# Row maxima handed over once a sequence instead of once a half, in a macaron block's attention

## The reference

```
x = x + 0.5 * ffn(layernorm(x))     # ternary weights, 1024 hidden units, silu(up) * gate
x = x + attn(layernorm(x))          # 16 heads of 16, 4 key/value groups, causal softmax
x = x + 0.5 * ffn(layernorm(x))
```

## Time and profile before

| | us |
|---|---|
| median of 3 runs | 615.65 |
| the runs | 616.25, 613.38, 615.65 |
| profiled execution, its own time | 613.52 |
| its span, first to last instruction | 611.8 |
| outputs of group 0 begin | 222.8 |
| outputs of chunk 6's first group begin | 397.8 |
| the attention's last output copy ends | about 441 |

### The profile page before, as it was taken

One profiled execution on the slowest core, in us unless ns is written; L12 is line 12 of the kernel. 1 busy time (PEld: TensorE's weight loads), 2 busy tenths in 40 slices (PEclk: granted clock), 3 DMA queues, 4 the chain that ended last, 5 costly groups with the idle time before them and its releaser, 6 DMA issues.

```text
span 611.8 us, 12440 instructions
## 1 busy us (share of the span) xinstructions
PE 566.2 (93%) x4276; PEld 344.7 (56%) x4276; DVE 484.4 (79%) x1850; ACT 413.2 (68%) x780; POOL 185.3 (30%) x231
## 2 busy tenths in 40 slices
PE   2879999999989889999899989998899999999998
PEld 2335566655656755666565656554445556666666
DVE  6797988889976789888988887888298687856654
ACT  4746656765645268898889888887866656665741
POOL 3022301101420234555555454557741011101100
DMA  9601101100203250514141414230111211212112
GB/s 313 211 19 34 19 18 35 35 19 18 36 0 96 46 143 6 140 36 108 54 91 56 90 56 90 81 65 5 36 35 34 53 53 36 66 49 59 35 35 70
DMA packets 69503, 37.90 MB, mean 62 GB/s; under 512 B 33856, under 2 KB 66880, under 8 KB 69440
## 3 DMA queue, kind: packets, MB, share of 16 engines
q1 hardware_dynamic: 69440, 37.11, 23.8%
HBM read 18.22 MB, written 10.49 MB: 47 GB/s over the span
## 4 chain that ended last, share of the span: by engine, by line
PE 76%; DVE 11%; ACT 8%; issue 2%; DMA 2%; SPq 1%; DVEq 0%; ACTq 0%
PE bank L1076 31%; PE bank L1088 16%; PE bank L1175 7%; PE bank L1239 6%; PE bank L1230 5%; PE bank L1202 5%; PE bank L1253 2%; PE bank L1244 2%; ACT shared L568 2%; DVE sm_out L938 2%; DVE hl L821 2%; DVE hid L806 2%; DVE stats L692 1%; PE bank L1213 1%; PE bank L1067 1%
## 5 line engine op out<-in xcount | busy, mean ns | idle before, releaser
L938 DVE CUSTOM_DVE_ANT_0 sm_out<-bank,mask 128x256 f16<-128x256 f32 (+1 forms) x512 | 153.0, 351 | 29.4 <-PE bank L1202 27.5
L464 ACT ACTIVATE silu<-bank,w_scale 128x512 f32<-128x512 f32 x128 | 87.4, 683 | 114.7 <-PE bank L1076 114.7
L806 DVE SCALAR_TENSOR_TENSOR hid<-silu,h_unit,bank 128x512 f32<-128x512 f32 x128 | 95.0, 742 | 64.5 <-ACT silu L464 64.1
L568 ACT ACTIVATE shared<-bank,qk_scale 128x512 f32<-128x512 f32 x192 | 121.3, 675 | 22.6 <-PE bank L1230 22.0
L1088 PE MATMUL bank<-wT_down,hh 128*128 128x256 f16 x512 | 118.3, 273 | 7.4 <-DVE hl L821 6.0
L1088 PE MATMUL bank<-wT_down,hl 128*128 128x256 f16 x512 | 118.2, 273 | 0.0
L821 DVE TENSOR_TENSOR hl<-hid,hh 128x512 f16<-128x512 f32 x128 | 103.2, 806 | 0.0
L1076 PE MATMUL bank<-xh,wT_up 128*128 128x512 f16 x256 | 98.0, 383 | 4.9 <-issue 2.5
L396 POOL TENSOR_TENSOR xnl<-xn,xnh 128x1024 f16<-128x1024 f32 x14 | 30.1, 2152 | 236.0 <-ACT xn L495 223.5
L1076 PE MATMUL bank<-xl,wT_up 128*128 128x512 f16 x256 | 98.0, 383 | 0.0
L1076 PE MATMUL bank<-xh,wT_gate 128*128 128x512 f16 x256 | 97.3, 380 | 0.8 <-DVE hid L806 0.7
(11 more groups left out here) (111 smaller groups left out, 751.5 us busy)
## 6 DMA issues: line engine op xcount, KB each, us to landing
q_st<-q_scratch SPq DMA_DIRECT2D x32, 256.0 KB
q_scratch<-q_hl SPq DMA_DIRECT2D x8, 512.0 KB, 3.1
out_dram<-x SPq DMA_DIRECT2D x7, 512.0 KB, 2.9
x<-in_x_dram SPq DMA_DIRECT2D x1, 3072.0 KB, 15.5
k_scratch<-k_hl SPq DMA_DIRECT2D x16, 128.0 KB, 2.4
k_st<-k_scratch SPq DMA_DIRECT2D x16, 128.0 KB
x<-in_x_dram SPq DMA_DIRECT2D x2, 512.0 KB, 4.3
shared<-in_w_up_t_dram SPq DMA_DIRECT2D x2, 512.0 KB, 6.6
```

The costliest lines, as they stand in the source:

```text
L464: act.activation(silu[:, e % 2, :], U[e % 2][:, :], ACT.Silu, scale=w_scale[:, 0:1]).then_inc(silu_ready, 1)
L568: act.activation(prob[:, place % 2, i, :], ST[(3 * place + i) % 2][:, :], ACT.Exp, scale=qk_scale[:, 4:5]).then_inc(exp_done, 1)
L806: dve.scalar_tensor_tensor(out=hid[:, e % 4, :], in0=silu[:, e % 2, :], scalar=h_unit[:, 0:1], in1=GT[e % 2][:, :], op0=ALU.mult, op1=ALU. ...
L938: ins = dve.tensor_tensor_reduce(sm_out[:, i, cols], SM[i][:, cols], mask[:, S - size:S], 1.0, MASKED, ALU.add, ALU.max, rowmax[:, seq_par ...
```

## The change

Everything that was done for 8 heads at g = 0 and g = 2 is done for 16 heads at g = 1. `HH` goes; `mx_hl` becomes [16, 2, 256], `mx_32` [16, 256], `mx_loaded` one semaphore. The transposes stand inside the group, after its `max_scores` and ahead of its third `scores`; ScalarE's copies stand between the second and the third exp; `outputs` now also waits for those copies; GpSimd's subtraction stands ahead of the selects. `max_scores` runs seven groups ahead. The projection pieces end one group earlier. Keys and the two query halves are written by separate steps, each as soon as it is ready, and the rows are cleared by the first of the four reads. The first maxima are turned over after the first feed-forward.

```diff
@@ SP @@
+            def write_queries(c, par, m):
+                sp.wait_ge(qkv_lo, 3 * c + m + 2)
+                sp.dma_start(q_scr[par, :, :, :, m]..., q_hl[:, :, m, :]).then_inc(scr_written, 16)
...
             def read_scratch(c, par, seq):
                 sp.wait_ge(scr_written, 16 * N_SCR * (c + 1))
+                sp.dma_start(q_st[64:66, par, :, cols], q_st[66:68, par, :, cols]).then_inc(loaded, 16)
                 for n in range(2):
...
-                sp.dma_start(q_st[64:66, par, :, cols], q_st[66:68, par, :, cols]).then_inc(loaded, 16)
...
-                        if g in (0, 2) and not (last and k == 3):
-                            load_max(b + 1, k + 1, g // 2)
+                        if odd and g == 0 and not last:
+                            write_queries(c + 2, par, 0)
+                        if g == 1 and not (last and k == 3):
+                            load_max(b + 1, k + 1)
+                        if not odd and g == 3 and not last:
+                            write_keys(c + 2, par)
                         if odd and g == 1 and not last:
-                            write_scratch(c + 2, par)
-                        if odd and g == 2 and not last:
+                            write_queries(c + 2, par, 1)
                             sp.wait_ge(st_ready, 3 * G * b)
                             read_scratch(c + 2, par, 0)
+                        if odd and g == 2 and not last:
                             sp.wait_ge(st_ready, 3 * G * (b + 1))
                             read_scratch(c + 2, par, 1)
@@ POOL, attention_pair @@
+                        if g == 1 and not end:
+                            max_rest(b + 1)
                         if not (end and g == 3):
                             causal(4 * b + g + 1, (g + 1) % 2)
-                        if g in (0, 2) and not end:
-                            max_rest(b + 1, g // 2)
@@ ACT, attention_pair @@
-                            if odd and g == 1:
+                            if odd and g == 0:
                                 query_high(c + 2, 1)
                         if not (end and g == 3):
-                            exps(*ahead, range(1, 3))
+                            exps(*ahead, range(1, 2))
+                        if g == 1 and not end:
+                            max_copy(b + 1)
+                        if not (end and g == 3):
+                            exps(*ahead, range(2, 3))
...
                         act.wait_ge(pv_ready, n + 1)
-                        if g in (0, 2) and not end:
-                            max_copy(b + 1, g // 2)
                         act.activation(oT[:, odd, g, :], PV[:, 0:S], ACT.Copy).then_inc(oT_ready, 1)
@@ ACT, attention @@
                 query_high(1, 0)
-                max_copy(0, 0)
+                max_copy(0)
                 query_high(1, 1)
-                max_copy(0, 1)
@@ DVE @@
-                            if odd and g == 1 and i == 2 and not last:
+                            if odd and g == 0 and i == 2 and not last:
                                 query_low(c + 2, 1)
...
-                for n in (4, 5):
+                for n in (4, 5, 6):
                     first_row_max(n)
-                row_max(6, 1, 2, 0)
+                row_max(7, 1, 3, 0)
@@ PE @@
-            def max_transposes(b, k, half):
-                pe.wait_ge(sm_done, 3 * (G * b + 2 * half + 2))
...
+            def max_transposes(b, k):
+                pe.wait_ge(sm_done, 3 * G * (b + 1))
...
-            PLACES = [..., (2, 0), (2, 1), (2, 2), (3, 0), (3, 1), (3, 2), (4, 0), (4, 2), (5, 0)]
+            PLACES = [..., (2, 0), (2, 1), (2, 2), (2, 3), (3, 0), (3, 1), (3, 2), (3, 3), (4, 0)]
...
-                            if g == 2:
+                            if g == 1:
                                 pe.wait_ge(st_loaded[1 - par][odd], 16 * N_ST * (pair + par + 1))
...
                             max_scores(*lead, range(2, 3))
+                        if g == 1 and not end:
+                            pe.wait_ge(oT_ready, n + 1)
+                            max_transposes(b + 1, k + 1)
                         projection(2)
...
                         pe.wait_ge(oT_ready, n + 1)
-                        if g in (0, 2) and not end:
-                            max_transposes(b + 1, k + 1, g // 2)
+                        if g == 1 and not end:
+                            pe.wait_ge(mx_ready, b + 2)
                         outputs(n, k, g)
...
             def attention():
                 pe.wait_ge(st_loaded[0][1], 16 * N_ST)
+                max_transposes(0, 0)
                 max_scores(4, 1, 0)
-                pe.wait_ge(res_done, NT + 2)
-                max_transposes(0, 0, 1)
                 val_transposes(1, (qkv_lo, 5))
+                max_scores(5, 1, 1)
+                max_scores(6, 1, 2)
                 scores(0, 0, 0, 0)
-                max_scores(5, 1, 1)
-                max_scores(6, 1, 2, range(0, 1))
+                max_scores(7, 1, 3, range(0, 1))
+                pe.wait_ge(res_done, NT + 2)
```

More of the change, by code:

```diff
@@ L46, in macaron_block @@
     NT = NC * TT
-    HH = H // 2
     VW = 32
@@ L334, in causal, with max_rest @@
                                    pattern=[[0, HPG], [1, P]], channel_multiplier=-1).then_inc(prob_ready, 1)
[L336 to L342 removed]
+            def max_rest(b):
+                pool.wait_ge(mx_ready, b + 1)
+                if b:
+                    pool.wait_ge(mx_loaded, 32 * b)
+                pool.tensor_tensor(mx_hl[:, 1, :], mx_32[:, :], mx_hl[:, 0, :], ALU.subtract).then_inc(mxlo_ready, 1)
             def attention_pair(pair, last):
@@ L552, in val_copy, with max_copy @@
                                ACT.Copy).then_inc(val_ready, 1)
-            def max_copy(b, half):
-                act.wait_ge(mxT_ready, 2 * b + half + 1)
-                if not (isinstance(b, int) and b == 0):
-                    act.wait_ge(mx_loaded[half], 32 * b)
-                maxima = FIRST_MT if isinstance(b, int) and b + half == 0 else MT
-                act.activation(mx_hl[:, half, 0, :], maxima[0:HH, :], ACT.Copy, scale=-1.0 / MAX_UNIT)
-                act.activation(mx_32[:, half, :], maxima[0:HH, :], ACT.Copy,
-                               scale=-1.0 / MAX_UNIT).then_inc(mx_ready, 1)
+            def max_copy(b):
+                act.wait_ge(mxT_ready, b + 1)
+                if b:
+                    act.wait_ge(mx_loaded, 32 * b)
+                maxima = MT if b else FIRST_MT
+                act.activation(mx_hl[:, 0, :], maxima[0:H, :], ACT.Copy, scale=-1.0 / MAX_UNIT)
+                act.activation(mx_32[:, :], maxima[0:H, :], ACT.Copy, scale=-1.0 / MAX_UNIT).then_inc(mx_ready, 1)
             def exps(n, place, parts):
@@ L974, in attention_pair @@
                     for g in range(G):
-                        lead = (4 * b + g + 6, (k + (g + 6) // 4) % 2, (g + 2) % 4)
-                        ahead = not (last and (k == 3 or (k == 2 and g >= 2)))
+                        lead = (4 * b + g + 7, (k + (g + 7) // 4) % 2, (g + 3) % 4)
+                        ahead = not (last and (k == 3 or (k == 2 and g >= 1)))
                         steps = {(0, 3): range(0, 4), (1, 0): range(4, 8),
@@ L1206, in max_scores @@
                     ins.then_inc(sm_ready, 1)
-            def max_transposes(b, k, half):
-                pe.wait_ge(sm_done, 3 * (G * b + 2 * half + 2))
-                if not (isinstance(b, int) and b == 0 and half == 0):
-                    pe.wait_ge(mx_ready, 2 * b + half)
+            def max_transposes(b, k):
+                pe.wait_ge(sm_done, 3 * G * (b + 1))
+                if b:
+                    pe.wait_ge(mx_ready, b)
                 for qt in range(QT):
-                    ins = pe.transpose((FIRST_MT if isinstance(b, int) and b + half == 0 else MT)[0:HH, qt * P:(qt + 1) * P], rowmax[:, k % 2, qt, half * HH:(half + 1) * HH],
+                    ins = pe.transpose((MT if b else FIRST_MT)[0:H, qt * P:(qt + 1) * P], rowmax[:, k % 2, qt, :],
                                        ident32[:, :])
@@ L1219, in scores @@
                 par, seq = k // 2 % 2, k % 2
-                if g % 2 == 0 and 0 in parts:
-                    pe.wait_ge(mx_loaded[g // 2], 32 * (b + 1))
+                if g == 0 and 0 in parts:
+                    pe.wait_ge(mx_loaded, 32 * (b + 1))
                 at, heads = seq * S, slice(HPG * g, HPG * (g + 1))
@@ L1265, in attention_pair @@
                         n, end = 4 * b + g, last and k == 3
-                        lead = (n + 6, k + (g + 6) // 4, (g + 2) % 4)
-                        ahead = not (end or (last and k == 2 and g >= 2))
+                        lead = (n + 7, k + (g + 7) // 4, (g + 3) % 4)
+                        ahead = not (end or (last and k == 2 and g >= 1))
                         def projection(place):
```

52 lines of the change are left out of this document (25 added, 27 removed).

## The result

| | before | after |
|---|---|---|
| median of 4 runs | 615.51 | 622.12 |
| the runs | 613.38 to 616.25 | 619.61 to 625.37 |
| profiled execution, its own time | 613.52 | 619.61 |
| its span | 611.8 | 617.9 |
| outputs of group 0 begin | 222.8 | 226.5 |

After / before is 1.0122 with a 95% interval of 1.0094 to 1.0149: slower by 1.2%. The forecast was 614.5, in a range of 609.5 to 618.7, so it was wrong in sign and in size.

What follows compares the result with a forecast made beforehand. TensorE (93% busy) was taken as the bound, with ScalarE the chain in odd g = 1 and g = 3. +3.7 - 2.9 - 0.5 - 1.4 = -1.1 us, profile 612.4, median 614.5; range 609.5 to 618.7.

Steps and rivals of the forecast that it cites:

- start: Ahead of the pairs: maxima copies delay query_high(1, 1), VectorE does one more group before the first pair; sum +3.7 us.
- chunks 0 to 5: Plain chunk saves 0.19, chunks 0, 2, 4 save 0.78 with the earlier last queries; together -2.9 us.
- chunk 6: Last pair: g = 1 costs +0.47 twice, the six other groups lose 1.41 in all; net -0.5 us.
- chunk 7: Last chunk: g = 1 gets +0.23, g = 2 loses 0.72 and 0.38, g = 3 loses 0.49; -1.4 us.
- Spare falls from 2.1 to 0.1. I take 0.: Strip reads wanted by TensorE at even g = 1: cost taken as 0, bounds 0 and 2.0 a chunk.
- the first rival: Strips arrive late: TensorE waits at even g = 1, chunks 1 to 6; 0.9 a chunk costs 5.4, giving 619.9; chance 0.18.
- The 0.59 goes ... I take the whole.: Chunks 0, 2, 4: query_low at odd g = 0 removes VectorE's 0.59 lateness; bounds 0 and 0.59.
- Odd g = 1, 3.49.: Outputs to outputs in odd g = 1, waiting for copies behind the second exp: 3.49 us, +0.23 against 3.26.
- The wait for the copies: At g = 1 outputs wait for ScalarE's maxima copies behind the second exp; odd +0.23, even 0.2 after TensorE's 3.48.
- The rival "does not bite": ScalarE far enough ahead at g = 1 that outputs needn't wait for the copies: 8.0 more saved, 606.5; chance 0.14.
- The landing of the maxima's load, 0.7 spare.: Odd sequence: load lands about 3.1 us after the copies, needed at g = 3 after 3.8, so 0.7 spare.
- The rival of a cheaper start: TensorE ends the feed-forward earlier or VectorE's extra group hides: half of 3.7 goes, 612.6; chance 0.13.

Runs made afterwards that it cites:

- k5: Changed kernel with 14 spare matmuls on TensorE ahead of the pairs, where it waits for row maxima; 618.74 us, ratio 1.0075 to the kernel before.
- k10: Changed kernel with SP writing the second query half at odd g = 0, ahead of its wait for the maxima; 618.27 us, ratio 1.0060.
- k11: Changed kernel with the maxima's copies in their old place, ahead of the PV copy, so outputs need not wait for them; 626.51 us, ratio 1.0195.
- k2: Changed kernel with SP issuing a chunk's second strip read only once the first strip has landed; 622.86 us, ratio 1.0134.
- k7: Changed kernel with the edits of k4, k1, k5 and k6 together; 610.22 us, ratio 0.9935 to the kernel before.
- k3: Changed kernel with the last four layernorm steps of chunks 0, 2, 4 moved from odd g = 1 to odd g = 2; 622.31 us, ratio 1.0134.
- k6: Changed kernel with the layernorm steps moved from the odd sequence of chunks 0, 2, 4 to the even sequence of chunks 1, 3, 5; 619.04 us, ratio 1.0096.
- k4: Changed kernel with the maxima copied ahead of the second exp instead of behind it; 615.61 us, ratio 1.0018 to the kernel before.
- k1: Changed kernel with ScalarE's query_high(1, 1) ahead of max_copy(0) before the pairs; 620.82 us, ratio 1.0085 to the kernel before.
- k12: Kernel before with only the new projection-piece places and the last queries' two parts at odd g = 0; 617.98 us, ratio 1.0055.
- k8: Kernel before with only the layernorm steps moved to the even sequence of chunks 1, 3, 5; 612.79 us, ratio 0.9972.

## Why the prediction was wrong, step by step

The miss is 7.2 in the profiled span (6.1 measured, -1.1 forecast) and 7.6 in the medians. By stretch:

| term | forecast | measured | miss |
|---|---|---|---|
| start | +3.7 | +3.8 | 0.1 |
| chunks 0 to 5 | -2.9 | +2.0 | 4.9 |
| chunk 6 | -0.5 | +1.0 | 1.5 |
| chunk 7 | -1.4 | -0.7 | 0.7 |

By cause, in the same profile: late strips 2.8; ScalarE's path to the outputs of g = 1, 2.0; VectorE 1.4; the maxima's load 0.5. The rest, 0.5, is small differences. Without the late strips the change would still have been slower in the profile, by 3.3, so the strips are the largest term and not the whole cause.

- **"Spare falls from 2.1 to 0.1. I take 0."** This is the step that failed in kind, and it was the first rival. For chunks 1 to 5 the spare was sized about rightly, and with 0.1 of it the first longer write made a strip late by 1.43 (chunk 5). For chunk 6 it was sized wrongly: the 10.7 us until TensorE wants the strip holds an even g = 0 of 4.49, put in for all six chunks, and chunk 6's takes 3.77. That makes its strip late by itself (0.63 in k5, where write and issue took their usual time), and 1.35 with the long issue. The two are 2.8 in all, and 2.8 is what k10 took away. It is less than the rival's 0.9 a chunk, since only two of seven strips were late. In the experiments that keep after's order of writes chunk 6 is always late, by 0.6 to 1.6; with it are late, k11 aside, none to three of the others, not the same ones from kernel to kernel. The rival's reason (strips in competition) was wrong: k2. Chunk 0 of k7 apart, what makes the others late is a write, a read or an issue that takes longer than usual, and each of these has a 16 KB instruction packet beside it (below).
- **"The 0.59 goes ... I take the whole."** VectorE was called just level with 3.4 us of work in 3.6. It was not: odd g = 2 is 3.13 where the steps run and 2.65 where not, 0.48 three times, 1.4. k3 moved it and gained nothing, k6 took it away and gained 1.4 in its intervals. Of the bounds 0 and 0.59, the right end was 0.11.
- **Odd g = 1, 3.49.** It took 3.70. From the PV copy on the sum holds (2.64 forecast, 334.05 - 331.43 = 2.62 measured). The miss is ahead of it: the PV copy was put right behind the outputs, 0.85 after their start, and came at 1.08, because ScalarE was still in the third exp of the group before. ScalarE had no slack from the start of that group, so each piece on it counted. Together with even g = 1 (3.77, 3.68 forecast) that is 6 x (0.21 + 0.09) = 1.8, and 0.2 more in the last pair (3.31 for 3.24 twice, 3.09 for 3.00).
- **The wait for the copies.** It was forecast to bite, and does. Its full price was not worked out against the obvious other order. k4 says it: 6.4 us by the ratios for one exp ahead of the copies; of the 6.0 in the profile 4.3 came directly and the rest through the maxima's load and the strips, for which the copies are the first link. The rival "does not bite" forecast 8.0 for no wait at all.
- **The landing of the maxima's load, 0.7 spare.** It was late twice, 0.5 in all: in odd g = 3 of chunk 5 (2.92), behind the issue of 1.5, after which it landed 2.7 and not 1.8 to 1.9 from that issue; and 0.28 in chunk 7, where GpSimd's subtraction took 1.17 and not 0.67, and the load is wanted 3.4 after the copies and not 3.8. The 2.0 us that the prediction draws from the Trainium skill (DMA: Bandwidth & Descriptors, Anatomy of one DMA) is given there for DMAs issued from GpSimd; these are issued from SP, and the usual 1.8 to 1.9 is near it. The rest of chunk 7's miss is g = 1 (3.09 for 3.00) and g = 2 (2.46 for 2.28), where TensorE waits for an exp.
- **The start, +3.7.** Right in the sum by luck and not in its parts. The mark came 0.95 earlier than before, and from it to the outputs it took +4.74; the surplus of 1.0 is about the low clock's price, 0.97 in k5, and the two errors cancel. In k2, k3 and k10 the same start cost 1.1 to 1.2 more, in k4, k6 and k11 as much as here within 0.2. The rival of a cheaper start fell; the wrong order in it was worth 1.2 by k1, not 2.1, since the low clock and the extra group then take over.
- **The transposes and the pieces.** Even g = 2, g = 3 and odd g = 0 (4.08, 4.08, 3.60) are as forecast (4.08, 4.09, 3.60); so are odd g = 3 (2.74 for 2.73) and even g = 0 (4.50 for 4.49). k12 shows the pieces' and queries' part alone to be a loss of 3.4, which the forecast had as 6 x 0.57 - 1.8 = +1.6. Of that difference 0.7 is again the VectorE term (odd g = 2 fell by 0.36 and not by 0.59, three times) and 0.8 the piece in even g = 3, which cost 0.66 there and not 0.53.

**Why a write takes 4.5.** SP does not stand still: it waits for the write to land, and the last sixteenth of the write moves late. Across the profiles of after and of the kernels made from it, six writes ahead of a strip's read take 3.0 to 4.5 instead of 2.3 (after, k2, k3, k5, k7, k11). Each has one 16 KB packet of queue 8, "instruction", begun 0.4 to 1.4 after its issue. In five of them 240 of the 256 packets of 1 KB go first, and the last 16 begin within 0.02 us of that packet's end; in k7 it begins ahead of the write's data, and the write takes the least (3.0). No write of 2.3 or 2.4 ahead of a read has a queue 8 packet begun in that span. Three strip reads on the chain of waits that land 4.9 to 5.6 after their last issue instead of 4.1 to 4.4 (k1, k5, k7) also have such a packet in or just before them. So has every SP issue of a plain DMA in the attention that takes over 1 us, of these kernels and of those made from the kernel before: the packet begins from 0.6 before the issue to 0.1 after its start. That a fetch of instructions holds up a sixteenth of the transfer is the reading that fits all of these, but it rests on coincidence in time: no run moves the fetches. What stays open is which engine's instructions they are, and why they fall where they do.

## What to carry to other kernels

Handing something over half as often removes instructions and gives away slack: before such a change, work out how late each consumer's data may be, for every stage and the last one too, whose groups are shorter, and treat a spare of 0.1 us under a transfer of 10 us as a late transfer with a chance, not as zero. If two halves of one bank tie a copy to the next matmuls, the copy's place in the copying engine's order can be the largest lever, as it was here (4.3 us directly, 6.4 in all), and it is to be priced in both orders. The same change with its copies ahead of both exps, the write a group earlier, the layernorm steps away from the full VectorE and TensorE kept busy at the start is 0.9% faster than before rather than 1.2% slower; 0.3% of that the kernel before can have from the layernorm steps alone (k8).

## What was not expected of the hardware

- TensorE's granted clock fell from 1.00 to 0.50 after two microseconds in which it was busy for 0.39, in a kernel at 92% over its span, and stayed there for about 7 us, in three other profiles of the same start for about 10; 14 spare matmuls of 512 columns prevented it, and the stretch was 0.8 to 2.2 us shorter.
- A 256 KB write lands 2.3 us after its issue, and 4.5 us with one 16 KB instruction packet amid it: 16 of its 256 packets begin only when that packet ends.
- A strip read of four DMAs lands 4.1 to 4.4 us after its last issue in after and k2, whether another such read follows it at once (4.20) or not (4.10).
- The kernel before itself had 0.3% in it: layernorm steps moved away from the last queries' work on VectorE (k8, 0.9972).
